# Score quads, stacked queries on the values' bank, the second half's Exp one slot later, and a third bank for gate and up in the last step

## What is computed

```python
x = x + attn_a(layernorm(x))                       # scan over tokens, 32 heads
x = x + ffn(layernorm(x))                          # sum over 8 experts
x = x + attn_b(layernorm(x))                       # softmax(q k^T / sqrt(8)), causal
x = x + ffn(layernorm(x))

def ffn(x):                                        # per expert, 128 -> 512 -> 128
    h = silu(x @ wg) * (x @ wu)
    acc = acc + h @ wd
```

## Time and profile before

| | |
|---|---|
| median of three runs | 1760.52 us (1751.52, 1760.52, 1761.1) |
| profiled execution, its own time | 1753.62 us |
| its span, first to last instruction | 1751.8 us |
| mean granted TensorE clock | 0.968 |
| PE busy, share of the span | 1557.5 us, 89% |
| DVE | 1177.6 us, 67% |
| ACT | 883.5 us, 50% |
| POOL | 723.5 us, 41% |

### The profile page before, as it was taken

The page is one execution under the profiler, slowest core; times in us unless marked ns, Lnnn a source line. Parts: engine busy times, 40 slices in busy tenths (PEclk is TensorE's granted clock), DMA queues, the critical chain, the costliest instruction groups (busy, mean ns, idle before and its releaser), DMA issues. The chain is left out here.

```text
span 1751.8 us, 23526 instructions
## 1 busy us (share of the span) xinstructions
PE 1557.5 (89%) x7720; PEld 1115.4 (64%) x7720; DVE 1177.6 (67%) x1943; ACT 883.5 (50%) x1552; POOL 723.5 (41%) x663
## 2 busy tenths in 40 slices
PE   3488998899898998978979999999899998999998
PEld 2266777677777776755656657657666576666665
DVE  5688787878787877685764755747557566474564
ACT  2245555555646564535545555465454554544544
POOL 2637354524344444211133444434344443343454
PEclk9689999999999999999999999999999999999999
DMA  6314533423333333322223333332333332332352
GB/s 192 108 50 153 199 144 137 153 108 144 145 144 145 144 136 117 144 80 101 109 76 109 141 106 115 110 115 109 115 108 109 115 110 107 115 144 97 127 186 79
DMA packets 36238, 216.68 MB, mean 124 GB/s; under 512 B 3476, under 2 KB 17301, under 8 KB 19733
## 3 DMA queue, kind: packets, MB, share of 16 engines
q1 hardware_dynamic: 36116, 215.18, 34.2%
HBM read 200.49 MB, written 15.47 MB: 123 GB/s over the span
## 5 line engine op out<-in xcount | busy, mean ns | idle before, releaser
L543 POOL TENSOR_TENSOR HL<-HF,HH 128x512 fp32r<-128x512 f32 x312 | 415.2, 1331 | 686.5 <-ACT HH L707 686.5
L1218 DVE SCALAR_TENSOR_TENSOR SG<-SG,gubank 128x512 f32<-128x512 f32 x288 | 197.2, 685 | 349.3 <-ACT SG L702 349.0
L873 PE MATMUL gubank<-XTH,W 128*128 128x512 f32 x875 | 379.9, 434 | 26.2 <-DVE HF L1235 7.8
L702 ACT ACTIVATE SG<-gubank 128x512 f32<-128x512 f32 x288 | 172.9, 600 | 424.9 <-PE gubank L875 424.9
L1235 DVE TENSOR_TENSOR HF<-SG,gubank 128x512 f32<-128x512 f32 x438 | 300.0, 685 | 119.3 <-PE gubank L875 56.6
L874 PE MATMUL gubank<-XTL,W 128*128 128x512 f32 x875 | 347.8, 398 | 0.0
L875 PE MATMUL gubank<-XTH,W 128*128 128x512 f32 x875 | 347.6, 397 | 0.0
L707 ACT ACTIVATE HH<-HF 128x512 fp32r<-128x512 f32 x512 | 320.7, 626 | 28.8 <-DVE HF L1235 28.0
L873 PEld LDWEIGHTS gubank<-XTH,W 128*128 128x128 f32 x875 | 167.8, 192 | 132.0 <-DVE HF L1235 37.7
L873 PE MATMUL dbank<-HH,W 128*128 128x512 f32 x512 | 220.3, 430 | 12.9 <-DVE HL L1224 11.9
L875 PE MATMUL dbank<-HH,W 128*128 128x512 f32 x512 | 203.7, 398 | 0.0
(11 more groups left out here) (231 smaller groups left out, 2115.0 us busy)
## 6 DMA issues: line engine op xcount, KB each, us to landing
W<-kept_w SPq DMA_DIRECT2D x120, 1536.0 KB, 6.5
kept_w<-W SPq DMA_DIRECT2D x8, 1536.0 KB, 6.2
X<-in_L_attn_a_x_dram SPq DMA_DIRECT2D x8, 256.0 KB, 5.7
WS<-in_L_ffn_Wg_dram SPq DMA_DIRECT2D x8, 256.0 KB, 6.5
WS<-in_L_ffn_Wu_dram SPq DMA_DIRECT2D x8, 256.0 KB, 6.7
WS<-in_L_ffn_Wd_dram SPq DMA_DIRECT2D x8, 256.0 KB, 6.9
out_dram<-X SPq DMA_DIRECT2D x8, 256.0 KB, 7.2
CST<-in_tables_dram SPq DMA_DIRECT2D x1, 896.5 KB, 5.3
```

The source lines that it names most:

```text
L543: g.tensor_tensor(HL[:, n % HRING, :], HF[:, n % HFRING, :], HH[:, n % HRING, :].bitcast(F32), ALU.subtract).then_inc(F.hl, 1)
L702: act.activation(SG[:, n % 2, :], gate_bank(n), ACT.Tanh, scale=0.5).then_inc(F.sil, 1)
L873: pe.matmul(dst, wh, xh, start=start, stop=False)
L1218: v.scalar_tensor_tensor(gated, gated, 1.0, gate_bank(n), ALU.add, ALU.mult).then_inc(F.half, 1)
```

## The change

Three things are changed.

1. The stacked queries of a sequence go to `abank`, one product in slot 7 and one in slot 9 (13 and 15 for the second sequence), in place of banks 0 and 1 of `quad`, both in slot 7 (13). So `quad` serves only quads between slots 0 and 22. Values, sums, ot, out and fturn move one slot later (the first "ot" and "out" stay), and with them their readers and the layer norm of the next step.
2. The second half's Exp of a column quad stands one slot later, right behind that slot's Tanh and ahead of HH; the first half's stays in its slot, behind HH.
3. In the last step gate and up rotate through three banks as in steps 0 to 6; `up` waits for `F.half` of the unit before and no longer for `F.mul`.

```diff
 B_CELL = {"turn": (-18, 1, 4), "q": (-8, 1, 1), "qs": (-8, 2, 2), "k": (-7, 1, 3), "ks": (-7, 2, 1), "v": (-5, 1, 3),
           "qst0": (-3, 1, 1), "qst1": (-3, 2, 2), "qst2": (-2, 1, 3), "qst3": (-2, 2, 1), "kst": (-1, 1, 2),
-          ("stack", 0, 0): (7, 1, 0), ("stack", 0, 1): (7, 2, 1), ("stack", 1, 0): (13, 1, 0),
-          ("stack", 1, 1): (13, 2, 1), ("pv", 0, 0): (16, 1, 4), ("pv", 0, 1): (18, 1, 4), ("sums", 0, 0): (20, 1, 4),
-          ("sums", 0, 1): (21, 1, 4), ("pv", 1, 0): (22, 1, 4), ("pv", 1, 1): (24, 1, 4), ("ot", 0): (25, 1, 0),
-          ("out", 0): (26, 1, 0), ("sums", 1, 0): (26, 2, 4), ("sums", 1, 1): (27, 1, 0), ("ot", 1): (28, 1, 4),
-          ("out", 1): (29, 1, 4), "fturn": (33, 1, 4)}
+          ("stack", 0, 0): (7, 1, 4), ("stack", 0, 1): (9, 1, 4), ("stack", 1, 0): (13, 1, 4),
+          ("stack", 1, 1): (15, 1, 4), ("pv", 0, 0): (17, 1, 4), ("pv", 0, 1): (19, 1, 4), ("sums", 0, 0): (21, 1, 4),
+          ("sums", 0, 1): (22, 1, 4), ("pv", 1, 0): (23, 1, 4), ("pv", 1, 1): (25, 1, 4), ("ot", 0): (25, 1, 0),
+          ("out", 0): (26, 1, 0), ("sums", 1, 0): (27, 1, 4), ("sums", 1, 1): (28, 1, 0), ("ot", 1): (29, 1, 4),
+          ("out", 1): (30, 1, 4), "fturn": (34, 1, 4)}
...
-            return fbank[2 * n % 3] if n < TANH else fbank[0]
+            return fbank[2 * n % 3] if n < TANH else fbank[0] if n < LAST else fbank[2 * (n - LAST) % 3]
...
-                if r == 31:
+                if r == 32:
                     norm_rs(n_f, TF, NT + t)
...
-            def exps(n, i):
-
-                for h in range(2):
-                    act.wait_ge(B.t_ready, 6 * n + 2 * i + h + 1)
...
+            def exps(n, i, h):
+
+                act.wait_ge(B.t_ready, 6 * n + 2 * i + h + 1)
...
+            def new_exps(slot, h):
+
+                for t, r in b_tiles(slot):
+                    for b in range(SPT):
+                        if r - 1 - h in COLS_AT[b]:
+                            exps(SPT * t + b, COLS_AT[b].index(r - 1 - h), h)
...
-                if r == 32:
+                if r == 33:
                     after(act, n_f.tp, NT + t)
                     norm_apply(n_f, TF, NT + t, XNF, lambda k: X[:, t, k, :])
-                if r == 34:
+                if r == 35:
                     ffn_hi(NT + t, sbank[bank_of(("b", t, "fturn"))])
...
                     gate_act(n)
+                new_exps(slot, 1)
                 n = unit_of(slot - 1)
                 if n is not None:
                     hidden_hi(n)
+                new_exps(slot, 0)
...
-                if n > TANH:
+                if TANH < n <= LAST:
                     pe.wait_ge(F.mul, n)
                 else:
                     after(pe, F.sil, n)
+                    after(pe, F.half, n - TANH)
...
-                        if r == B_CELL["sums", b, a][0] + (b == 1 and a == 0):
+                        if r == B_CELL["sums", b, a][0]:
                             gather_sums(n, a, sbank[bank_of(("b", t, ("sums", b, a)))])
...
-                if r == 30:
+                if r == 31:
                     v.wait_ge(B.done, SPT * (t + 1))
                     norm_stats(n_f, TF, NT + t, lambda i: X[:, t, i, :])
-                if r == 34:
+                if r == 35:
                     norm_lo(n_f, NT + t, sbank[bank_of(("b", t, "fturn"))], XTH[:, t % 2, :], XTL[:, t % 2, :])
```

More of the change, by code:

```diff
@@ L101 @@
 TANH = (NT - 1) * UNIT
+LAST = (2 * NT - 1) * UNIT
 POOL_LOW = (0, 2, 4, 6, 8, 10, 12)
@@ L236, in gate_bank @@
         def gate_bank(n):
-            return fbank[2 * n % 3] if n < TANH else fbank[0]
+            return fbank[2 * n % 3] if n < TANH else fbank[0] if n < LAST else fbank[2 * (n - LAST) % 3]
         def up_bank(n):
-            return fbank[(2 * n + 1) % 3] if n < TANH else fbank[1]
+            return fbank[(2 * n + 1) % 3] if n < TANH else fbank[1] if n < LAST else fbank[(2 * (n - LAST) + 1) % 3]
         X = sb("X", [P, NT, SUB, C])
@@ L775, in side_a @@
                     ffn_hi(t, sbank[bank_of(("a", t, "fturn"))])
-            def exps(n, i):
-                for h in range(2):
-                    act.wait_ge(B.t_ready, 6 * n + 2 * i + h + 1)
-                    after(act, B.pv, 2 * (n - 1) + 1 if i == 1 else 2 * n)
-                    at = NG * i + 2 * h
-                    act.activation(PT[:, at:at + 2, :], quad[:, 2 * h:2 * h + 2, :], ACT.Exp,
-                                   scale=DB ** -0.5).then_inc(B.t_used, 1)
+            def exps(n, i, h):
+                act.wait_ge(B.t_ready, 6 * n + 2 * i + h + 1)
+                after(act, B.pv, 2 * (n - 1) + 1 if i == 1 else 2 * n)
+                at = NG * i + 2 * h
+                act.activation(PT[:, at:at + 2, :], quad[:, 2 * h:2 * h + 2, :], ACT.Exp,
+                               scale=DB ** -0.5).then_inc(B.t_used, 1)
+            def new_exps(slot, h):
[3 more added lines that the diff above has]
+                            exps(SPT * t + b, COLS_AT[b].index(r - 1 - h), h)
             def side_b(t, r):
@@ L809, in side_b @@
                     n = SPT * t + b
-                    for i in range(3):
-                        if r == COLS_AT[b][i] + 1:
-                            exps(n, i)
                     for z in range(2):
@@ L886, in gate @@
                     after(pe, F.mul, n if n == TANH else n - 1)
+                if n == LAST + 1:
+                    pe.wait_ge(B.o, 2 * SPT * NT)
                 w = x % WRING
```

## The result

The changed kernel takes 1708.0 us (median of four executions, 1703.4 to 1708.4), the kernel before, run beside it, 1759.5 (four, 1751.5 to 1761.1). The ratio is 0.971, with a 95% interval of 0.968 to 0.974. The profiled execution of the changed kernel took 1708.1 us, its span 1706.3, which is 45.5 us under the span of before. Forecast were 1707 us, or 1714 by the level of the medians, and 46.7 less.

The account below looks back on a forecast made before the run. PE, busy 89% of 1751.8 us, bounds the kernel, so its waits count. Gains 26.5 + 24.0 + 9.6 + 10.6 less losses 2, 17.2 and 4.8 give 46.7: 1707 us (1714 by the median's level), range 1686 to 1737.

Parts of the forecast that it names:

- Slots 7 to 9: First sequence's stacks: the 2.8 us wait for the quad's bank goes, window 12.58 to 10.2 us, 26.5 us less in all.
- Rival (b): Slots 4 to 12: DVE sets the pace, gates wait instead, 26.5 us of gain lost, 1733; chance 0.12.
- Slots 13 to 15: Second sequence's stacks no longer wait for Exp; with new waits 10.5 us in all, 24.0 us less over the steps.
- Slots 16 to 25: Same work reordered: 2.3 us of new Exp waits against 3.5 of old ones, 1.2 less a tile, 9.6 us.
- 1.3 that modelled ends hide: Slots 16 to 25: part of 3.5 us of old waits a tile, beside 1.2 seen idle and 0.9 in bare slots.
- The step boundary: Slots 32 to 35: next step's norm a slot later, first gate waits for XTL; 2.4 us more six times, 17.2 lost.
- The clock: At step boundaries: PE idles 2.7 us, so the clock falls in half of six, 1.6 us each, 4.8 lost.
- The last step: Gate and up on three banks: units of 2.04 us, 63.6 in place of 74.24 us, 10.6 less.
- rival (c): Last step: POOL sets the pace because HL follows itself; 10.6 us less gain, 1718; chance 0.07.
- Rival (a): abank becomes the queue: five hand-overs a tile uncovered, 26 us more, 1733; chance 0.09.
- Rival (d): Late second-half Exp: PE waits for ACT at six places a tile, 115 us more, 1822; chance 0.07.
- the forecast's own sign of being wrong: Gates waiting for SG in slots 4 to 12, Exp waits past a microsecond, or XTL's wait far from 2.7 us.

## Why the forecast came out as it did

**Slots 7 to 9** (-26.5 forecast, -26.4 measured): steps 9 to 14 as worked out, 10.2 forecast and 10.25 measured (step 8 9.16 where 9.3 was put, step 7 9.98 where about 10.25), with the second stack's wait of 0.38 us for the residual where 0.45 was put. The stacks alone on the kernel before give the same window, so that moving them is the cause is shown, not only argued. Rival (b) would have shown gates waiting for SG: DVE has 8.82 us of work in these 10.25, and the only gate that waits for SG in slots 7 to 12, that of slot 12, does so for 0.1 us.

**Slots 13 to 15** (-24.0, -26.8): 10.15 where 10.5 was forecast. The turn does wait for XN, 0.67 us idle; but the quad behind it in slot 14 loses next to nothing to the late Exp, which ends with down of that slot (it starts 0.38 us behind down's last product, 0.33 where both Exps stand together). The term of 0.4 was put on top of 0.8 though both run in the same slot: the wait for XN gives Exp the time. The second pair was not moved alone. In the kernel with both Exps together, which has the moved stacks and no late half, these slots take 10.99 us where 13.09 stood before; the late half gives 0.84 more.

**Slots 16 to 25** (-9.6, -7.0): the new waits were sized well (0.22 idle at three quads, 0.91 at q; one late Exp in place of six takes back 2.1 us a tile of the 2.3 forecast). What fails is the other side, the 3.5 us of old waits: 2.1 + 0.66 (38.25 to 37.59) is 2.8. Which of its pieces was too large isn't shown by itself; the "1.3 that modelled ends hide" is the one that no row had shown. A part is arithmetic: the pieces as listed add up to 3.4 of old waits and 2.4 of new ones, 1.0 a tile or 8.0 us, and not to 3.5, 2.3 and 9.6.

**The step boundary** (+17.2, +20.8): six boundaries cost 2.56 us each where 2.4 was forecast, the wait for XTL 2.53 idle where 2.7 was. The term that failed is the gap ahead of step 8, +4.0 where 1.2 was put. There the forecast counted only the extra reduction in front of XTL. The timeline of the changed kernel, the turn and step 8's first gate, and below it the same two in the kernel before:

```profile
862.90 0.63 PE L924 MATMUL abank<-CST,XNF 128*128 128x128 f32 x4 [3.06 <-ACT XNF L694]
868.61 0.79 PE L879 MATMUL gubank<-XTH,W 128*128 128x512 f32 x1 [2.69 <-DVE XTL L1221]
```

```profile
873.18 0.63 PE L915 MATMUL abank<-CST,XNF 128*128 128x128 f32 x4 [0.39 <-ACT XNF L693]
878.29 0.50 PE L873 MATMUL gubank<-XTH,W 128*128 128x512 f32 x1 [1.76 <-DVE XTL L1212]
```

The four slots between the steps have no gate or up to fill them, so a norm that comes a slot later is waited for at the turn as well: 2.67 us more there, 0.93 at the gate, and the clock falls besides (0.85 in that window).

**The clock** (+4.8, +6.9): it falls behind three of the six boundaries, as forecast, at 1.5 us each; the fourth fall, 2.3 us behind the gap, was left out. That the falls behind the six boundaries come from the wait for XTL is shown: in the four kernels with 2.53 to 2.56 us of idle PE there the clock falls in 13 of 24 places, in the seven with 1.42 or less in none of 42. Which of the six it hits changes from kernel to kernel, so that it was three is luck. For the fall behind the gap this isn't shown: it comes also in four kernels whose gate there waits 1.76 us or 1.77, as long as in the kernel before, where the clock held.

**The last step** (-10.6, -10.4): units of 2.04 us, PE busy all the time; rival (c) is out. **Rival (a)** counted six more users of `abank`; the four stacks are the only ones, and of their hand-overs one is seen waiting, for 0.38 us. **Rival (d)** had its point of decision at 1.0 us more a place: the longest wait for the late Exp is 0.9 idle at q (1.17 between gate starts, against 1.1 forecast), 0.2 at the quads. So the forecast's own sign of being wrong, a wait for Exp over a microsecond, was set below what it expected at q. It was the right thing to weigh, since that wait is what the better kernels give back.

The forecast was right in time and, part by part, in mechanism. Four of its terms are off by 2 to 4 us each, three to the worse and one to the better, 4.4 us of gain lie in stretches that it put at nothing, and the time is taken from an execution that was 6 us faster than the median run beside the changed kernel: that 1707 stands so close to 1708 is luck. Its range is added up loosely too: the cases named give about 1688 to 1740, not 1686 to 1737. What it didn't see is that two parts of the change cost more than they need: the norm's slot (27 us with the clock) and five of the six late Exps (some 15).

## What to carry to other kernels

When an instruction waits for a bank, ask whether it needs that bank at all, and whether the wait names the part of it that the instruction needs. Moving it to a bank whose users have a unit's matmuls between them gave back all that the wait had cost in its slots; a part of the clock was lost again behind other waits. When a whole table of slots is shifted to make room, shift only the entries that need the room: the followers' latency (here the next step's norm) shows up undiminished wherever PE has nothing else queued. A later place for an instruction on a shared engine should be given to the one position that gains from it, and a wait for a split result should name the half that it needs.
